# Second attention of a two-layer network: the causal mask moves from TensorE into VectorE's row maximum, and the order of a step changes

## The reference

```python
y = jnp.einsum('bnd,hde->bhne', x, Wkqv) + bkqv[None, :, None, :]
k, q, v = y[..., :Dm], y[..., Dm:2 * Dm], y[..., 2 * Dm:]
A = jnp.einsum('bhnd,bhmd->bhnm', q, k) / jnp.sqrt(jnp.float32(Dm))
A = jnp.where(mask[None, None], A, -jnp.inf)      # mask: lower triangle
A = jax.nn.softmax(A, axis=-1)
sa = jnp.einsum('bhnm,bhmd->bnhd', A, v).reshape(Bm, Nm, Dm)
```

## Time and profile before

| | us |
|---|---|
| median of 3 runs | 2656.59 |
| lowest and highest run | 2652.44, 2658.57 |
| the profiled execution's own time | 2639.07 |
| its span | 2637.3 |
| TensorE busy | 2377.5 |
| VectorE busy | 1886.6 |
| ScalarE busy | 1562.1 |
| GpSimd busy | 1022.7 |

### The profile page before, as it was taken

One profiled execution on the slowest core, in us unless ns is written; L12 is line 12 of the kernel. 1 busy time (PEld: TensorE's weight loads), 2 busy tenths in 40 slices (PEclk: granted clock), 3 DMA queues, 4 the chain that ended last, 5 costly groups with the idle time before them and its releaser, 6 DMA issues. The chain is left out here.

```text
span 2637.3 us, 67465 instructions
## 1 busy us (share of the span) xinstructions
PE 2377.5 (90%) x17172; PEld 1690.3 (64%) x17173; DVE 1886.6 (72%) x5258; ACT 1562.1 (59%) x4145; POOL 1022.7 (39%) x1980
## 2 busy tenths in 40 slices
PE   5999999987999999999999999999989964999970
PEld 3676777765666666666666666666657753777750
DVE  6888888844777777777777777777744553666658
ACT  2555555554777777777777777777743322444445
POOL 5666666651222222222222222222215664444432
PEclk9999999998999999999999999999975556999985
DMA  1101111101000000000000000000041111111125
GB/s 31 32 25 32 32 32 32 32 19 37 0 0 0 0 0 0 0 0 0 0 0 0 0 0 0 0 0 0 0 119 64 61 58 46 52 53 51 52 66 160
DMA packets 78015, 71.60 MB, mean 27 GB/s; under 512 B 10621, under 2 KB 70538, under 8 KB 77084
## 3 DMA queue, kind: packets, MB, share of 16 engines
q1 hardware_dynamic: 69262, 53.65, 7.0%
q0 software_dynamic: 8704, 17.39, 2.0%
HBM read 36.32 MB, written 22.62 MB: 22 GB/s over the span
## 5 line engine op out<-in xcount | busy, mean ns | idle before, releaser
L887 PE MATMUL ps_s<-xT_all,qm 128*128 (+2 forms) x2048 | 695.9, 448 | 0.8 <-ACT qm L955 0.8
L1005 DVE SCALAR_TENSOR_TENSOR restT<-ps_t,leadT 128x512 f16<-128x512 f32 (+3 forms) x1024 | 498.3, 487 | 259.9 <-ACT leadT L970 259.9
L970 ACT ACTIVATE leadT<-ps_t 128x512 f16<-128x512 f32 (+3 forms) x1024 | 422.4, 441 | 311.2 <-PE ps_t L901 311.1
L962 ACT ACTIVATE p<-ps_s,neg_max 128x512 f32<-128x512 f32 (+3 forms) x1024 | 483.3, 525 | 32.8 <-DVE neg_max L997 4.6
L997 DVE TENSOR_REDUCE neg_max<-ps_s 128x1 f32<-128x512 f32 (+3 forms) x1024 | 471.4, 481 | 30.6 <-PE ps_s L889 30.6
L901 PE MATMUL ps_t<-ident,p 128*128 128x128 f32 x2560 | 416.8, 277 | 19.3 <-issue 17.4
L887 PEld LDWEIGHTS ps_s<-xT_all,qm 128*128 128x128 f32 x2048 | 309.9, 191 | 156.5 <-issue 118.7
L840 POOL CAST v_parts<-v_all 128x36 bf16 (+1 forms) x256 | 56.5, 221 | 875.6 <-PE ps_o L913 875.6
L901 PEld LDWEIGHTS ps_t<-ident,p 128*128 128x128 f32 x2560 | 278.9, 141 | 179.6 <-issue 179.4
L879 PE MATMUL ps_qm<-xT_all,m_head 128*128 (+1 forms) x512 | 271.7, 612 | 0.5 <-ACT mb_all L947 0.5
L266 POOL TENSOR_TENSOR pv_prod<-probs,kv 128x2048 f32<-128x2048 f32 x64 | 259.6, 4079 | 0.1
(11 more groups left out here) (216 smaller groups left out, 4196.6 us busy)
## 6 DMA issues: line engine op xcount, KB each, us to landing
row_in<-rows_dram SPq DMA_DIRECT2D x136, 64.5 KB, 1.8
y<-results SPq DMA_DIRECT2D x32, 256.0 KB, 3.3
xT<-in_xT SPq DMA_DIRECT2D x32, 128.0 KB, 2.1
xres<-in_xT SPq DMA_DIRECT2D x32, 128.0 KB, 2.1
x_all<-x SPq DMA_DIRECT2D x32, 128.0 KB, 2.0
xT_all<-x2T SPq DMA_DIRECT2D x32, 128.0 KB, 2.0
x_all<-x SPq DMA_DIRECT2D x16, 256.0 KB, 2.5
out_x<-x SPq DMA_DIRECT2D x16, 256.0 KB, 2.2
```

Source lines behind the costliest of these rows:

```text
L887: pe.matmul(ps_s[i][:, 0:n], qm[j][:, i * P:n], xT_all[:, bass.ds(sequence(u) * S, n)], start=True, stop=False)
L962: act.activation(probs[i][:, :], ps_s[i][:, 0:(i + 1) * P], ACT.Exp, bias=neg_max[:, i:i + 1]).then_inc(probs_ready[i], 1)
L970: act.activation(leadT[i][:, :], ps_t[i % 2][:, 0:(i + 1) * P], ACT.Copy, scale=RAISE)\
L1005: dve.scalar_tensor_tensor(out=restT[i][:, :], in0=ps_t[i % 2][:, 0:(i + 1) * P], scalar=RAISE, in1=leadT[i][:, :], op0=ALU.mult, op1=ALU. ...
```

## The change

The mask matmuls go, and with them the bf16 identity and mask. A float32 mask of 512 columns is built instead, 0 in its first 384 columns and the triangle in the last 128. `row_max` becomes `mask_and_max`: one instruction of VectorE computes -(scores + mask), writes it over the scores in PSUM and hands out the minimum of each row. The exponential takes it with a scale of -1. The wait for the scores stands in an instruction of its own.

The transposed blocks form three groups: block 3; blocks 2 and 0; block 1. Groups 0 and 2 share one bank, group 1 has the other. So `copy_lead` and `take_rest` each run three times in a step (512, 512 and 256 columns), not four. The scores of blocks 0 and 1 share one bank, and one semaphore. The products with the values give one semaphore for all blocks. Each engine has a new order per step.

```diff
-        ident16 = sb("ident16", [P, P], BF16)
-        mask16 = sb("mask16", [P, P], BF16)
+        mask = sb("mask", [P, S])
...
+        groups = ((3,), (2, 0), (1,))
+        width = [sum(i + 1 for i in group) * P for group in groups]
+        group_of = {3: (0, 0), 2: (1, 0), 0: (1, 3 * P), 1: (2, 0)}
...
+        ps_s = (ps_low[:, 2 * P:3 * P], ps_low[:, 0:2 * P], ps_s2[:, 0:3 * P], ps_s3[:, :])
+        ps_t = (ps_t0, ps_t1, ps_t0)
...
                 def scores(u, j, i):
                     k = 2 * u + j
                     pe.wait_ge(qm_sb, k + 1)
-                    when(pe, probs_ready[i], k)
-                    n = (i + 1) * P
-                    pe.matmul(ps_s[i][:, 0:n], qm[j][:, i * P:n], xT_all[:, bass.ds(sequence(u) * S, n)],
-                              start=True, stop=False)
-                    pe.matmul(ps_s[i][:, i * P:n], ident16[:, :], mask16[:, :], start=False, stop=True)\
-                        .then_inc(scores_ps[i], 1)
-
-                def turn(u, j, i):
+                    for n in ((1, 0) if i == 1 else (i,)):
+                        when(pe, probs_ready[n], k)
+                        mm = pe.matmul(ps_s[n], qm[j][:, n * P:(n + 1) * P],
+                                       xT_all[:, bass.ds(sequence(u) * S, (n + 1) * P)], start=True, stop=True)
+                    mm.then_inc(scores_ps[i], 1)
+
+                def turn(u, j, g):
                     k = 2 * u + j
...
+                    if g == 0:
+                        when(pe, rest_ready[2], k)
+                    if g == 1:
+                        when(pe, rest_ready[1], k)
+                    if g == 2:
+                        pe.wait_ge(rest_ready[0], k + 1)
+                    for i in groups[g]:
+                        pe.wait_ge(probs_ready[i], k + 1)
+                        at = group_of[i][1]
+                        for n in range(i + 1):
+                            mm = pe.transpose(ps_t[g][:, at + n * P:at + (n + 1) * P], probs[i][:, n * P:(n + 1) * P],
+                                              ident[:, :])
+                    mm.then_inc(pT_ps[g], 1)
...
                 def step(u, j, nxt, last, this):
                     b = before(u, j, 1)
                     if last:
-                        turn(*b, 3)
-                        turn(*b, 2)
+                        turn(*b, 0)
                     if this:
                         scores(u, j, 3)
+                    if last:
+                        turn(*b, 1)
+                    if this:
                         scores(u, j, 2)
                     if last:
-                        turn(*b, 1)
+                        turn(*b, 2)
                     if nxt:
                         queries(*before(u, j, -1))
-                    if last:
-                        turn(*b, 0)
                     if this:
                         scores(u, j, 1)
-                        scores(u, j, 0)
                     if last:
-                        for i in reversed(range(B)):
-                            weighted_values(*b, i)
+                        weighted_values(*b)
...
                 def exponentials(u, j, i):
                     k = 2 * u + j
+                    if i == 1:
+                        act.wait_ge(max_ready[0], k + 1)
                     act.wait_ge(max_ready[i], k + 1)
-                    when(act, pT_ps[i], k)
-                    act.activation(probs[i][:, :], ps_s[i][:, 0:(i + 1) * P], ACT.Exp,
-                                   bias=neg_max[:, i:i + 1]).then_inc(probs_ready[i], 1)
...
+                    when(act, pT_ps[group_of[i][0]], k)
+                    act.activation(probs[i][:, :], ps_s[i], ACT.Exp,
+                                   bias=neg_max[:, i:i + 1], scale=-1.0).then_inc(probs_ready[i], 1)
...
                 def step(u, j, nxt, last, this):
                     b = before(u, j, 1)
                     if last:
-                        copy_lead(*b, 3)
-                        copy_lead(*b, 2)
+                        copy_lead(*b, 0)
                         copy_lead(*b, 1)
                     if this:
                         exponentials(u, j, 3)
+                    if last:
+                        copy_lead(*b, 2)
+                    if this:
                         exponentials(u, j, 2)
-                    if last:
-                        copy_lead(*b, 0)
                     if nxt:
                         copy_queries(*before(u, j, -1))
...
-                def row_max(u, j, i):
+                dve.wait_ge(consts_made, 1)
+
+                def mask_and_max(u, j, i):
+
                     k = 2 * u + j
-                    dve.wait_ge(scores_ps[i], k + 1)
-                    dve.tensor_reduce(neg_max[:, i:i + 1], ps_s[i][:, 0:(i + 1) * P], AX_X, ALU.max,
-                                      negate=True).then_inc(max_ready[i], 1)
-
-                def take_rest(u, j, i):
+                    n = (i + 1) * P
+                    wait_alone(dve, scores_ps[max(i, 1)], k + 1, passed_dve)
+                    dve.tensor_tensor_reduce(out=ps_s[i], in0=ps_s[i], in1=mask[:, S - n:S],
+                                             scale=-1.0, scalar=3e38, op0=ALU.add, op1=ALU.min,
+                                             accum_out=neg_max[:, i:i + 1]).then_inc(max_ready[i], 1)
...
                 def step(u, j, nxt, last, this):
                     b = before(u, j, 1)
                     if last:
-                        take_rest(*b, 3)
+                        take_rest(*b, 0)
                     if this:
-                        row_max(u, j, 3)
+                        mask_and_max(u, j, 3)
+                    if last:
+                        take_rest(*b, 1)
+                    if this:
+                        mask_and_max(u, j, 2)
                     if last:
                         take_rest(*b, 2)
                     if this:
-                        row_max(u, j, 2)
-                    if last:
-                        take_rest(*b, 1)
-                        take_rest(*b, 0)
-                    if this:
-                        row_max(u, j, 1)
-                        row_max(u, j, 0)
+                        mask_and_max(u, j, 1)
+                        mask_and_max(u, j, 0)
                     if last:
                         normalise(*b)
```

More of the change, by code:

```diff
@@ L761, in attention1 @@
         out_sum, recip = sb("out_sum", [P, B * PV]), sb("recip", [P, B])
-        ps_s = [ctx.enter_context(nc.psum_tensor(f"ps_s{i}", [P, S], F32)) for i in range(B)]
-        ps_t = [ctx.enter_context(nc.psum_tensor(f"ps_t{i}", [P, S], F32)) for i in range(2)]
+        ps_low, ps_s2, ps_s3, ps_t0, ps_t1 = (
+            ctx.enter_context(nc.psum_tensor(name, [P, S], F32)) for name in ("ps_low", "ps_s2", "ps_s3", "ps_t0", "ps_t1"))
+        ps_s = (ps_low[:, 2 * P:3 * P], ps_low[:, 0:2 * P], ps_s2[:, 0:3 * P], ps_s3[:, :])
+        ps_t = (ps_t0, ps_t1, ps_t0)
+        ps_m = (ps_low, ps_s2, ps_s3, ps_t0)
         ps_qm = ctx.enter_context(nc.psum_tensor("ps_qm", [P, S], F32))
@@ L817, in _ @@
             def _(pool):
-                pool.memset(mask16[:, :], 0.0).then_inc(consts_zeroed, 1)
-                pool.tensor_copy(ident16[:, :], ident[:, :]).then_inc(consts_made, 1)
+                pool.memset(mask[:, :], 0.0).then_inc(consts_zeroed, 1)
                 pool.wait_ge(consts_zeroed, 1)
-                pool.affine_select(out=mask16[:, :], in_=mask16[:, :], compare_op=ALU.is_ge, fill=MASKED,
-                                   base=0, pattern=[[-1, P]], channel_multiplier=1).then_inc(consts_made, 1)
+                pool.affine_select(out=mask[:, 3 * P:4 * P], in_=mask[:, 3 * P:4 * P], compare_op=ALU.is_ge,
+                                   fill=MASKED, base=0, pattern=[[-1, P]], channel_multiplier=1)\
+                    .then_inc(consts_made, 1)
                 pool.wait_ge(m_sb, H // 4)
@@ L863, in _ @@
                     for h in range(4 * g, 4 * g + 4):
-                        mm = pe.matmul(ps_s[g][:, (h % 4) * P:(h % 4 + 1) * P], wq[:, h * P:(h + 1) * P],
+                        mm = pe.matmul(ps_m[g][:, (h % 4) * P:(h % 4 + 1) * P], wq[:, h * P:(h + 1) * P],
                                        wk[:, h * P:(h + 1) * P], start=True, stop=True)
@@ L905, in weighted_values @@
-                def weighted_values(u, j, i):
-                    k = 2 * u + j
[L907 to L916, removed]
+                    for n in ((1, 0) if i == 1 else (i,)):
+                        when(pe, probs_ready[n], k)
+                        mm = pe.matmul(ps_s[n], qm[j][:, n * P:(n + 1) * P],
+                                       xT_all[:, bass.ds(sequence(u) * S, (n + 1) * P)], start=True, stop=True)
@@ new lines, in weighted_values @@
+                def weighted_values(u, j):
+                    k = 2 * u + j
+                    pe.wait_ge(v_parts_ready, 3 * (k + 1))
+                    when(pe, out_summed, k)
+                    for i in (3, 2, 0, 1):
```

(12 more changed lines are left out.)

51 lines of the change are left out of this document (21 added, 30 removed).

## The result

The changed kernel takes 2625.04 us, median of 4 runs (2623.35 to 2626.48), the kernel of before in the same rounds 2654.52 us. The ratio is 0.9888, 95% interval 0.9868 to 0.9908: 29 us or 1.1% faster, where 67 us were forecast. The direction and the range held; the size was off by more than half.

A forecast was written before the change was run, and what follows sets the result against it. TensorE's order was taken to bound the second attention at 5.00 us a step; its 4.66 to 4.78 and chains of 4.65 and 4.69 gave 4.74. 256 x (5.00 - 4.74) = 67 us off 2656.59 gives 2590 us, range 2560 to 2652.

The forecast's parts named there:

- TensorE's row: TensorE's own work per step of the second attention without mask matmuls: 4.66 us at best, 4.78 if today's distances stay.
- The other two have air: In the second attention, VectorE and ScalarE have slack: busy 153.47 and 148.02 of 200 us, against TensorE's 197.13.
- The fused pass: VectorE's mask, minimum and write-back: streaming costs 0.01 us more than the row maximum, handing out the minimum 0.10 per pass.
- The separate wait: Wait instruction before each VectorE pass: 0.07 us over a usual wait for block 1, bound 0.23; three others find scores done.
- two chains close on themselves: In the new order, one chain through block 3's scores and queries' copy takes 4.65 us, one through block 0's exponential 4.69.
- the 4.69 and the 4.74: Per step of the second attention: 4.69 us is the longer of two priced chains, 4.74 us the step length forecast.
- The loop's turn: Cost of the second attention's loop turning, 0.13 us per step over the 5.00, left as it is.
- The signs of being wrong: TensorE waits for block 0's exponential or queries' copy over 0.1 us a step; pass much over 0.9; block 2's scores still 0.69.
- waits eat most of it: Rival, chance 0.22: slower handoffs or separate wait make the second chain 4.85 to 4.94 us; gain 15 to 38 us.
- become the bound by its amount of work: Rival, chance 0.13: fused pass at half rate makes VectorE's step 5.5 us with waits; 128 us more, 2785 us.
- the likeliest case: Second attention's steps take 4.66 to 4.83 us, total time 2566 to 2613 us; chance 0.55.

The follow-up runs named there:

- the hybrid: Changed kernel with a bank of its own for the third transposed group, and blocks 1 and 0 back to TensorE masks and plain maximum: 2579.77 us, ratio 0.9779.

## Why the prediction was right or wrong

*TensorE's row*: right. Without a wait the step from 1003.00 to 1007.72 took 4.72 us, between 4.66 and 4.78, and block 2's scores 0.65. That this row would set the time failed.

*"The other two have air"*: wrong. No wait of TensorE was on record in the earlier trace rows, but the ring of VectorE and ScalarE in the old order lay 0.05 us under its step; the run without masks in the old order shows it.

*The fused pass*: the streaming part (690 ns against 681) and the accumulator read were right. The Trainium skill (VectorE: DVE Perf Modes, section "Two Vector instructions with no wait between them") says that such an op is two instructions, and the rows agree: 160 reads of 142 ns in the stretch. The 0.10 us of delay per pass was about its size, 0.06 for block 3 (0.74 us from the pass's start to the read's end, against 0.68) and 0.11 for block 0. As occupancy it was too much: the follower starts together with the read, and the passes over blocks 1 and 0 hold VectorE for 0.60 us, where the plain maxima behind the same wait take 0.54.

*The separate wait*: mis-sized. I took 0.11 us from the scores' end to the pass; it is 0.19. In the run without masks the wait alone costs 0.080 us a step.

*The new order, "two chains close on themselves"*: this step failed. A third one closes as well. It runs through group 0's copy, which has to stand behind the short exponentials, then the rest and the shared bank; neither of the two chains has that copy in it. By the prediction's own prices it comes to 0.63 (short exponentials) + 0.62 (copy) + 0.73 (rest) + 0.23 (group 2) + 0.86 (queries) + 0.65 + 0.16 (scores 1 and 0 to their end) + 0.11 (wait) + 0.81 (passes) + 0.04 = 4.84 us, above the 4.69 and the 4.74, for a gain of some 41 us. Measured it is 4.93 and 5.11 us by turns. In the shorter round the wait takes 0.08 more than priced, the passes 0.07 less, group 2's transposes 0.04 more and the rest of the chain 0.04; the longer one adds 0.18, half of it in the queries. Opening it by a bank or by the queries' place took 0.07 us off the step, and then the ring over two steps (4.92 us) held.

*The loop's turn*: "I leave it as it is" failed too. It was the term of 0.13 us a step, and it fell to some 0.02 in the changed kernel. So the forecast of 4.87 us a step had 0.28 us too little for the ring (5.02 against 4.74) and 0.11 too much for the turn.

*Luck*: that the time fell as forecast is not to the reasoning's credit. The 67 us were to come from the masks, whose move gives nothing once the order is new and loses 18 us in the old one; the gain comes from the turn, which the prediction left alone. The range held because it reached up to 2652.

*The signs of being wrong*: one came true, TensorE's wait for the queries' copy at 0.12 us a step (4.7 us in 40). The larger wait, 0.45 us a step for the rest of group 0, was not among them.

*The rivals*: "waits eat most of it", with 2619 to 2642 us, is what happened, by another chain than the one priced. VectorE did not become the bound by its amount of work. One bound of the likeliest case is off by its own sum: a step of 4.66 us gives 2570 us, not 2566.

## What to carry to other kernels

An engine that waits for nobody does not show that the others have air: follow each engine's queue around, from the last instruction of a step to the same one in the next, and add up every ring, also those without the busiest engine and those over two steps. Price an operation that moves to another engine by the delay that it puts between producer and consumer, not by its busy time; keep it off the block that closes the ring, as the hybrid does. When two changes come together, run each alone: here one gave everything and the other nothing in the new order and a loss in the old.

## What was unexpected of the hardware

The end of a loop's body costs TensorE 0.44 us between two matmuls when the rest that its last products need is ready 0.2 us before the last of them, 0.31 in the changed kernel, where it is ready 0.4 us before (1022.83 to 1023.14), and 0.19 where it is 0.6. That its instruction stream can then run ahead of the engine is my reading; the two runs with eight steps (15 and 3 us) bear out the sizes only.

A product of 512 float32 columns takes 0.86 us to the next start, but in some steps 0.96 (the queries at 1010.71, followed at 1011.67). It happens behind transposes that had waited, but not always: the queries at 1015.73, behind such transposes too, took 0.87. Why is open.

VectorE's accumulator read has a row of 0.14 us and holds up its follower hardly at all. Where the follower starts 0.09 us after it (1017.09 behind 1017.00), it is a rest that waited for ScalarE's copy, which ended at 1017.06.
